# A gated product moved from VectorE to GpSimd in the first stage of a four-stage kernel, with normalisation on ScalarE

## What is computed

```python
x = x + _L0_xattn_ref(_layernorm(x, axis=-1), ctx_768, ...)   # cosine of every token with every context token
x = x + _L0_ffn_ref(_layernorm(x, axis=-1), ...)              # experts

# _L0_xattn_ref
v = einsum('bsd,hd->bsh', visual_features, Wv) + bv
t = einsum('bsd,hd->bsh', text_features, Wt) + bt
dots = einsum('bih,bjh->bij', v, t)
denom = maximum(norm(v)[:, :, None] * norm(t)[:, None, :], EPS)
return dots / denom
# _L0_ffn_ref: 8 experts of width 64, the best 2 of the best 2 groups of 4, one shared expert of width 128
topk_idx, topk_w = _gate(xf, gate_w, gate_bias)
g = silu(einsum('th,ehi->tei', xf, w_gate));  u = einsum('th,ehi->tei', xf, w_up)
experts_y = einsum('tei,eih->teh', g * u, w_down)             # then the chosen two, times topk_w
shared = silu(x @ sw_gate) * (x @ sw_up) @ sw_down
```

## Time and profile before

| | us |
|---|---|
| median of 3 runs | 955.29 (953.72 to 956.67) |
| profiled execution, its own time | 956.91 |
| its span, first to last instruction | 954.9 |
| first stage: last addition of the stage starts at | 255.70 |
| VectorE busy in the whole span | 661.3 (69%) |
| TensorE busy in the whole span | 751.5 (79%) |

### The profile page before, as it was taken

One profiled execution on the slowest core, in us unless ns is written; L12 is line 12 of the kernel. 1 busy time (PEld: TensorE's weight loads), 2 busy tenths in 40 slices (PEclk: granted clock), 3 DMA queues, 4 the chain that ended last, 5 costly groups with the idle time before them and its releaser, 6 DMA issues. The chain is left out here.

```text
span 954.9 us, 26276 instructions
## 1 busy us (share of the span) xinstructions
PE 751.5 (79%) x10100; PEld 556.5 (58%) x10100; DVE 661.3 (69%) x1809; ACT 395.2 (41%) x746; POOL 227.0 (24%) x366
## 2 busy tenths in 40 slices
PE   3579889887637887888888428778764999999998
PEld 2345555554415665666676305556554788888886
DVE  4478888986446887888888347888644656666653
ACT  2122122222113554555555325566532554555553
POOL 4333333320083022201000475335001111111100
PEclk9958898978956999999999658999995999999999
DMA  3000000520112211221110000000000000000000
GB/s 93 20 20 21 18 4 17 129 40 11 23 46 77 70 42 41 69 71 52 50 53 13 9 0 4 3 5 4 3 4 2 1 13 11 11 11 11 11 11 12
DMA packets 33081, 26.41 MB, mean 28 GB/s; under 512 B 9740, under 2 KB 29912, under 8 KB 32984
## 3 DMA queue, kind: packets, MB, share of 16 engines
q1 hardware_dynamic: 29944, 24.07, 9.5%
q10 hardware_dynamic: 3040, 0.98, 0.4%
HBM read 13.51 MB, written 7.34 MB: 22 GB/s over the span
## 5 line engine op out<-in xcount | busy, mean ns | idle before, releaser
L1777 PEld LDWEIGHTS bank<-w2r,hme 128*128 128x128 f32 x1024 | 132.1, 191 | 16.3 <-ACT hme L1618 2.1
L1777 PE MATMUL bank<-w2r,hme 128*128 128x128 f32 x1024 | 135.6, 276 | 0.5 <-DVE Xq L1720 0.5
L1618 ACT ACTIVATE hme<-bank,b 128x512 f32<-128x512 f32 x128 | 86.6, 688 | 95.8 <-PE bank L97 95.7
L785 ACT ACTIVATE P<-bank 128x512 f32<-128x512 f32 x128 | 76.8, 600 | 95.9 <-PE bank L956 95.8
L1720 DVE SCALAR_TENSOR_TENSOR Xq<-bank,wgte,Xq 128x128 f32 (+1 forms) x256 | 72.0, 344 | 51.9 <-PE bank L1777 38.4
L886 DVE TENSOR_SCALAR bank<-bank 128x512 f32<-128x512 f32 x128 | 89.0, 696 | 27.0 <-PE bank L947 26.9
L894 DVE TENSOR_REDUCE mx<-bank 128x4 f32<-128x512 f32 x128 | 87.1, 681 | 1.4 <-PE bank L939 1.2
L956 PE MATMUL bank<-mT,negsel 128*128 128x128 f16 x512 | 51.0, 223 | 44.5 <-DVE bank L886 41.9
L350 ACT ACTIVATE sg<-bank 128x512 f32<-128x512 f32 x40 | 23.9, 598 | 128.2 <-PE bank L581 99.0
L956 PEld LDWEIGHTS bank<-mT,negsel 128*128 128x128 f16 x512 | 32.1, 99 | 55.5 <-issue 40.9
L767 POOL TENSOR_TENSOR inv_sum<-inv_sum,dn 128x16 f32<-128x16 f32 x32 | 7.1, 221 | 203.2 <-DVE dn L915 203.2
(11 more groups left out here) (376 smaller groups left out, 1787.6 us busy)
## 6 DMA issues: line engine op xcount, KB each, us to landing
cross_q<-qh SPq DMA_DIRECT2D x24, 128.0 KB
K<-cross_k SPq DMA_DIRECT2D x96, 32.0 KB
Q<-cross_q SPq DMA_DIRECT2D x8, 384.0 KB, 3.6
X<-in_x SPq DMA_DIRECT2D x8, 256.0 KB, 2.8
Xq<-X SPq DMA_DIRECT2D x32, 64.0 KB
cross_k<-kh SPq DMA_DIRECT2D x16, 128.0 KB
Yq<-Y SPq DMA_DIRECT2D x32, 64.0 KB
out_x<-Xq SPq DMA_DIRECT2D x32, 64.0 KB, 1.7
```

Of the source, the lines that this page charges most:

```text
L785: act.activation(P[j][:], TB[j % 2][:], ACT.Exp, scale=SCALE).then_inc(s["p_ready"], 1)
L1618: act.activation(hm[:, p % HR], UP[p % RING][:], ACT.Gelu_apprx_tanh, bias=b1[:, p:p + 1]).then_inc(s["gelu"], 1)
L1777: last = pe.matmul(Y[e % 2][:, cols], hm[:, p % HR, cols], w2r[:, p], start=(p % 2 == 0 and i == 0), stop=(p % 2 == 1), skip_group_check=True)
```

## The change

- The product by the routing weight comes first and is GpSimd's: ScalarE copies bank `WB` to a new tile `wide`, GpSimd makes `su = sg * wide`, VectorE makes `hm = su * UP`. The shared expert's block is as before.
- The banks are dealt out anew: one gate bank, two up banks by turns, and a signal of its own for each of the three products (`g_psum`, `u_psum`, `w_psum`).
- The normalisations A and B go to ScalarE, as `x * rs + (-mean * rs)`, at the beginning of block 0 of the next step. GpSimd's `root` makes the two numbers for it, with two more small instructions.
- The ranking takes two instructions instead of four: a difference, and one comparison of it with a table that is 0 or -2e-38.
- The loop over steps 1 to 4 is written out.

```diff
@@ GpSimd, step(g), ahead of cosines(g + 2, p) @@
+                    if has(g) and p < NBLK - 1:
+                        k, j = NBLK * g + p, (NBLK - 1) * g + p
+                        pool.wait_ge(s["sg_ready"], k + 1)
+                        pool.wait_ge(s["wide_ready"], j + 1)
+                        after(pool, s["hm_ready"], k - 1)
+                        pool.tensor_tensor(su[:, k % 2, :], sg[:, k % 2, :], wide[:, j % 2, :], ALU.mult
+                                           ).then_inc(s["su_ready"], 1)
...
@@ ScalarE @@
+            def normalise(k, g):
+                act.wait_ge(s["rs" + k], g + 1)
+                for i in range(GB):
+                    last = act.activation(xn[k][:, i, :], xg(g)[:, i, :], ACT.Identity, bias=rs[k][:, 3, i:i + 1],
+                                          scale=rs[k][:, 1, i:i + 1])
+                last.then_inc(s["xn" + k], 1)
...
                     if has(g):
-                        act.wait_ge(s["gu_psum"], k + 1)
-                        after(act, s["hm_ready"], before(k, p) + 1)
-                        act.activation(sg[:, p % 2, :], GP[p % 2][:], ACT.Silu).then_inc(s["sg_ready"], 1)
+                        act.wait_ge(s["g_psum"], k + 1)
+                        after(act, s["hm_ready"], k - 1)
+                        act.activation(sg[:, k % 2, :], GP[:], ACT.Silu).then_inc(s["sg_ready"], 1)
+                    if p == 0 and has(g + 2):
+                        normalise("A", g + 2)
+                    if p == 0 and has(g + 1):
+                        normalise("B", g + 1)
                     if has(g + 2):
                         prep(g + 2, p)
                     if has(g + 1):
                         route(g + 1, p)
+                    if has(g) and p < NBLK - 1:
+                        j = (NBLK - 1) * g + p
+                        act.wait_ge(s["w_psum"], j + 1)
+                        after(act, s["su_ready"], j - 1)
+                        act.activation(wide[:, j % 2, :], WB[:], ACT.Copy).then_inc(s["wide_ready"], 1)
...
@@ VectorE @@
-                    dve.tensor_tensor(room[:, 0], other, own, ALU.is_gt)
-                    link(dve.tensor_tensor(room[:, 1], other, own, ALU.is_equal))
-                    link(dve.tensor_tensor(room[:, 2], room[:, 1], tie, ALU.mult))
-                    link(dve.tensor_tensor(room[:, 1], room[:, 0], room[:, 2], ALU.add))
+                    link(dve.tensor_tensor(room[:, 0], other, own, ALU.subtract))
+                    link(dve.tensor_tensor(room[:, 1], room[:, 0], least, ALU.is_gt))
...
                     if has(g):
-                        dve.wait_ge(s["sg_ready"], k + 1)
-                        after(dve, s["down_psum"], k - NBLK + 1)
+                        dve.wait_ge(s["u_psum"], k + 1)
                         if p < NBLK - 1:
-                            dve.tensor_tensor(su[:, i, :], sg[:, i, :], UP[:], ALU.mult).then_inc(s["su_ready"], 1)
                             dve.wait_ge(s["su_ready"], (NBLK - 1) * g + p + 1)
-                            dve.tensor_tensor(hm[:, p, :], su[:, i, :], WB[:], ALU.mult).then_inc(s["hm_ready"], 1)
+                            after(dve, s["down_psum"], k - NBLK + 1)
+                            dve.tensor_tensor(hm[:, p, :], su[:, i, :], UP[i][:], ALU.mult).then_inc(s["hm_ready"], 1)
@@ GpSimd, root(k, g) @@
                 pool.tensor_scalar(rs[k][:, 0, :], mv[k][:, :, 1], 1.0, LN_EPS, ALU.mult, ALU.add
                                    ).then_inc(s["eps" + k], 1)
+                pool.tensor_scalar(rs[k][:, 2, :], mv[k][:, :, 0], -1.0, None, ALU.mult).then_inc(s["eps" + k], 1)
+                pool.tensor_tensor(rs[k][:, 1, :], rs[k][:, 0, :], half[:, 0:GB], ALU.pow).then_inc(s["eps" + k], 1)
+                pool.tensor_tensor(rs[k][:, 3, :], rs[k][:, 2, :], rs[k][:, 1, :], ALU.mult).then_inc(s["rs" + k], 1)
@@ TensorE @@
-                after(pe, s["sg_ready"], before(k, p) + 1)
-                split_product(pe, GP[i][:], [w[:, 0, p, :] for w in w0], x)
-                after_alone(pe, s["hm_ready"], k, s["carrier"])
-                last = split_product(pe, UP[:], [w[:, 1, p, :] for w in w0], x)
+                after(pe, s["sg_ready"], k)
+                split_product(pe, GP[:], [w[:, 0, p, :] for w in w0], x).then_inc(s["g_psum"], 1)
+                after(pe, s["hm_ready"], k - 1)
+                split_product(pe, UP[k % 2][:], [w[:, 1, p, :] for w in w0], x).then_inc(s["u_psum"], 1)
+            def weight(g, p):
+                if p == 0:
+                    pe.wait_ge(s["eT_ready"], g + 1)
                 if p < NBLK - 1:
-                    last = pe.matmul(WB[:], pick[:, p, :], tok(eT, g), start=True, stop=True)
-                last.then_inc(s["gu_psum"], 1)
+                    after(pe, s["wide_ready"], (NBLK - 1) * g + p)
+                    pe.matmul(WB[:], pick[:, p, :], tok(eT, g), start=True, stop=True).then_inc(s["w_psum"], 1)
```

More of the change, by code:

```diff
@@ L179, in layer0 @@
         su = sb("su", [128, 2, N])
+        wide = sb("wide", [128, 2, N])
         hm = sb("hm", [128, NBLK, N])
@@ L201, in sweep @@
         def sweep(eng, step):
-            for g in range(-3, 1):
-                step(g)
-            with eng.Fori(1, G - 3) as g:
-                step(g)
-            for g in range(G - 3, G):
+            for g in range(-3, G):
                 step(g)
@@ L227, in load @@
                 wait_alone(sp, s["c_loaded"], 16 * (g + 1), s["carrier"])
-            over_groups(sp, load, 0, G - 1)
+            for g in range(G):
+                load(g)
             for tile, source in keep["moves"]:
@@ L379, in stats @@
                 last.then_inc(s["mv" + k], 1)
-            def normalise(k, g):
-                wait_alone(dve, s["rs" + k], g + 1, s["carrier"])
-                for i in range(GB):
-                    last = dve.tensor_scalar(xn[k][:, i, :], xg(g)[:, i, :], mv[k][:, i, 0:1], rs[k][:, 1, i:i + 1],
-                                             ALU.subtract, ALU.mult)
-                last.then_inc(s["xn" + k], 1)
             steps = 0
```

34 lines of the change are left out of this document (16 added, 18 removed).

## The result

The changed kernel took 992.28 us (median of 4 runs, 988.93 to 995.21) against 954.54 of the kernel before (4 runs): ratio 1.0395, 95% interval 1.0355 to 1.0436. It is slower, as forecast, but by 37.7 us and not by 24, and it lies outside the range of 965 to 990.

A forecast was written before the change was run, and what follows sets the result against it. It took a first-stage ring of engine hand-overs as the bound: 0.6 + 4.4 + 23 (five turns) - 4.3 (drain) = +23.7 us, profiled 956.9 to 980.6, forecast 979 us after a median adjustment; range 965 to 990.

The forecast's parts named there:

- the turn: First-stage stretch between starts of VectorE's `n2`, once per step; forecast 30.8 us against 26.14, with five full ones.
- E: Link from the low half of `xa` to the first gate instruction; forecast 6.8 us in place of 4.71.
- D: Link from the transposes of `xnB` on TensorE to the low half of `xa`; forecast 3.97 us against 1.18.
- the half turn: Stretch ahead of the five full ones, with experts only in its second half; forecast +4.4 us.
- the relief of VectorE: Rival: VectorE's relief decides and stretches shrink until TensorE sets them; 926 us, chance 0.07.
- the cheap ring: Rival: same dependency ring, no GpSimd block at the gate, shorter statistics link, better drain; about 968 us, chance 0.15.
- the ring with a slow TensorE: Rival: transposes and t products at 1.2 GHz lengthen each turn by 1 to 2 us; 985 to 991, chance 0.15.
- A: Link from `n2` to `wm`, with block 3's product; forecast 5.7 us, as long as before (5.69).
- C: Link from the end of statistics B to the transposes of `xnB`; forecast 3.2 us against 2.96.
- The drain: Last stretch of the first stage, emptying the pipeline; two up banks break a serial chain, forecast -4.3 us.
- F: Link from the first gate instruction to the next `n2`; forecast 5.9 us against 5.95, including 1.1 for GpSimd's block.
- B: Link from `wm` to the end of statistics B; forecast 5.2 us against 5.65.

The follow-up runs named there:

- e9: Changed kernel with VectorE's `wm` ahead of `hm` in block 3 instead of behind it; 985.22 us.
- e11: Changed kernel with unread filler matmuls on TensorE: 12 ahead of the wait for `xnA`, 5 each ahead of those for the squares and the addition; 984.75 us.
- e8: Changed kernel with unread filler matmuls on TensorE, 12 ahead of the wait for `xnA` and 8 ahead of the wait for the addition; 989.88 us.
- e2: Changed kernel with both products back on VectorE, without `wide`; normalisation on ScalarE, short ranking, banks and loop as changed; 951.09 us.
- e3: Changed kernel with normalisations and root of before, on VectorE and GpSimd; product, banks and ranking as changed; 979.22 us.
- e10: Kernel before with only its loops written out, banks and signals as before; 944.00 us.
- e4: Changed kernel with product, normalisation and ranking of before; new banks, signals and written-out loop stay; 937.46 us.
- e5: Changed kernel with product and normalisation of before; short ranking, new banks, signals and written-out loop stay; 930.94 us.
- e6: Changed kernel reordered: ScalarE's copy right behind the silu, GpSimd's block 1 product behind the squares, VectorE's `hm` last in its block; 969.08 us.
- e7: Changed kernel with copy behind the silu, GpSimd's block 1 product behind the squares, `hm` last, and normalisation and root of before; 956.16 us.

## Why the prediction was wrong in size

**Right.** The direction, and the mechanism: `hm` waits for GpSimd, GpSimd for ScalarE's copy at the end of its block, and VectorE, relieved, stands idle behind these waits for almost half of the turn. E was forecast at 6.8 and measured at 6.72, part by part as in the sum (1.88 to the end of `cT`, 0.93 to `vt`, GpSimd 1.27), so that is no luck; D at 4.0 and 4.32 (the 0.3 is the transposes of `xnB`, which took 1.12 after a wait of 0.90 and not the 0.66 of the earlier trace rows), GpSimd's product at 1.27 and 1.265 (mean of 20), the half turn at +4.4 and +5.4, the blocks of the last step at 2.4 and, from 279.51 to 284.42, 2.4 to 2.5. Of the rivals, the relief of VectorE (926) and the cheap ring (968) are excluded; the ring with a slow TensorE (985 to 991) came nearest; but of the transposes and t products of which it spoke only those of `xnB` were slow, and most of its price fell on A. Its premise had been read wrongly, too: in the walked turn TensorE waits for more than 1 us in one place, not in five (2.14 ahead of the broadcast; the others are 0.53 to 0.78, and all of its idle time is 26.14 - 21.95 = 4.2). Of the signs named, the third stretched gate instruction did not come: the same two were stretched further. Two of its signs of being wrong did come: links A and C grew, and TensorE's clock in the five turns was 0.84, not 0.9.

By the profiled execution the first stage grew by 40.0 us (its last addition from 255.70 to 295.74), where the sum had 23.7. These are the steps that failed:

1. **A: "That gives 5.7, as long as before; the broadcast on TensorE (1.96) runs beside it." It was 6.85 to 7.40.** I priced the product of block 3 from the end of `dg`, as if its operand were ready. It wasn't: `wide` waits for the `pick` matmul, which stands on TensorE behind a down product that waits for the addition and then, with seven more, runs at the 1.2 GHz level. e9 shows that `hm` of block 3 was what held `wm` (A 4.8 once it stands behind), e11 and the one turn of e8 that the low clock is 1.0 to 1.7 of it (A 5.45 to 6.13 against a mean of 7.1), e2 and e3 that it comes with GpSimd's product. The place of `hm` and the low clock lie on the same chain, so their shares can't be added. In the changed kernel this is +1.2 to 1.7 a turn, 7.1 in all against the forecast.
2. **C: "0.9 to 1.2 against 1.12. I take 3.2." It was 4.13.** The nearest row, 0.31 for one activation, was a copy. The four with a scale and a bias per partition take 0.482 each and 1.65 together; VectorE's four took 1.12. That is 0.6 of the 0.9. The other 0.3 is root B, which stands behind the longer root A on GpSimd and ends 2.39 after the statistics. e3 undoes both: C 2.6. The Trainium skill has this price, in "ScalarE: Activation LUTs", section "What ACT_TABLE_LOAD costs": 186 ns and 0.833 ns for each element of a partition, 93 ns more for each operand that is a pointer, and 93 ns of overlap between neighbours. The estimate from it is 0.479 for one and 1.64 for four, and the trace agrees with both (0.482 and 1.65). The prediction did not use it; by that estimate C would have come out 0.6 longer.
3. **The drain: "-4.3". It grew by 1.8** (from 49.61 to 51.36, to the end of the last addition). The gain is there and larger than I had it: 8.0 us by the banks (e10 to e4). But the product's longer way runs through each step of the drain as it does through a turn, and I had charged it for the last `hm` alone. It costs 9.0 to 11.0 there (e2 to the changed kernel, e5 to e3).
4. **The prologue, at nothing, took 1.4.** The first `n2` starts at 27.67 to 28.45 in the seven kernels with normalisation on ScalarE, and at 26.33 to 27.32 in the six without it.
5. **The loop written out, at nothing.** e10 is 8.7 us shorter than before in the stage, of which 3.2 are the two turns with a low clock and may not be the loop's. I had lowered my link B without naming the loop (5.2; measured 4.81), and in e10 B is 4.80 with nothing else changed.
6. **F, 5.9 against 5.22, and B, 5.2 against 4.81**, were too dear. In F the block by GpSimd was there (1.33 and 1.20 for two instructions that took 1.04 and 0.97 before), but cost 0.5 and not 1.1, since VectorE came late to it. In e6 and e7, where it comes in time, it costs all of it: F is 7.15. The rule on the shared ports that the prediction cited from the Trainium skill, "SBUF — State Buffer", section "SBUF: two separate sides", agrees with the rows of e6: `sfc`, whose two inputs are in SBUF, is held through GpSimd's products. Its price depends on when the two meet.

Against the forecast the prologue has +1.4, the first two turns +1.4, the five turns +7.5 (161.54 - 131.08 - 23) and the drain +6.1: together 16.3 before rounding, which is 40.0 - 23.7. The 7.5 of the five turns hides errors that cancel: A, C and D were 7.1, 4.6 and 1.7 too cheap, and F, B and E 3.4, 2.0 and 0.4 too dear. The rest of the kernel gave 5.6 back, within what it varies by itself.

**What the parts are worth,** by the start of the last addition, from kernel to kernel (before, e10, e4, e5, e2, after): the loop -8.73, banks and signals -4.03, ranking -9.55, normalisation on ScalarE +20.57, the product on GpSimd +41.78. The sum is +40.04. In the other order (e5 to e3, e3 to after) the product is +48.8 and the normalisation +13.5. Each is a difference of single executions, and the first three contain the turns with a low clock, which come and go between e10, e4 and e5 (3.3 us of the -9.55 are E going from 6.26 back to 4.60 in two turns). The prediction had also said of the ranking's second half that it "brings nothing". No run takes the short ranking out of the changed kernel, but VectorE waits 3.24 us there, four times the 0.8; without the product the ranking counts, and A is 4.88 in e5 against 5.5 in e4.

**Open.** Why TensorE's clock is low in block 0 in some turns and not in others (E 6.24 to 6.36 in two turns each of before and e4, none of e10 and e5), and so how much of the 8.7 is the loop's. Why the clock rises earlier in e9. Of the product's 41.8 to 48.8, the order of the three queues explains 21.4 (after to e6); of the 20.4 left (e6 against e2) F has 8.1, five times 1.63, A 5.6 and the drain 5.2. How A and the drain divide between the longer way over two more engines, the later addition and the low clock was not tried.

## What to carry to other kernels

Work taken off the busiest engine helps only if what replaces it does not stand in front of that engine's next instruction: walk the ring with the new waits in it, and for each operand of a moved instruction go back to the queue that produces it, not to the last thing that you know is ready. Charge a longer chain in every step in which it runs, those of the drain too. And measure the parts of a compound change apart: this one had in it 22 us of gain in the stage (banks, loop, ranking, by e5), which the product and the normalisation ate up.

## What the runs showed of the hardware that was not expected

- With a loop of four steps written out, the five full turns took 123.31 us in place of 131.08 with the same instructions (e10); 3.2 of the 7.8 us are two turns with a low clock, which a kernel without the loop (e4) can have as well.
- An activation of 128 columns takes 0.482 us with scale and bias from a tile, 0.31 as a copy.
- Two GpSimd products back to back hold a VectorE instruction of 0.2 us for 2.42 us: it doesn't get in between them (e6). Between the two squares of `sq` it sometimes does: in the kernel before the two gate instructions took 1.04 and 0.97 beside them, one square each, and in e6 the first was held by both (2.03).
- TensorE's work costs up to twice its time at the lower of its two levels: the eight matmuls of a down product 2.05 against 1.05. In the changed kernel that was so behind a wait of 1.56 us, but also behind one of 0.59. Fillers raised the granted clock of the turns from 0.84 to 0.94 and won 6.8 us of 161.5 (e11), but where the clock was low when they began, eight of them took 3.2 to 3.6 us themselves, and in two turns they cost more than they gave (A 8.9 and 8.3 in e8).
